# Fused adapter MLP, residual and gated FFN: the last down weight block, the first down parts and the first loads take other places

## The reference

```python
# x [8, 128, 512]; one of 16 adapters of rank 16 for each batch, SCALE = 0.5
gate = x @ W_gate.T + SCALE * (x @ A_gate[i].T) @ B_gate[i].T      # 1376 wide
up   = x @ W_up.T   + SCALE * (x @ A_up[i].T)   @ B_up[i].T
act  = silu(gate) * up
y    = act @ W_down.T + SCALE * (act @ A_down[i].T) @ B_down[i].T  # 512 wide
nx   = y * rsqrt(mean(y * y) + 1e-5) * ln_w
out  = x + (silu(nx @ gate_w.T) * (nx @ up_w.T)) @ down_w.T        # 1792 wide
```

## Time and profile before

| | us |
|---|---|
| median of 3 runs | 421.85 (421.34 to 421.91) |
| the profiled execution | 418.57 |
| its span in the trace | 416.8 |
| TensorE busy | 407.8 (98%) |
| VectorE busy | 320.4 (77%) |
| ScalarE busy | 234.4 (56%) |
| GpSimd busy | 12.4 (3%) |

### The profile page before, as it was taken

The page is one execution under the profiler, slowest core; times in us unless marked ns, Lnnn a source line. Parts: engine busy times, 40 slices in busy tenths (PEclk is TensorE's granted clock), DMA queues, the critical chain, the costliest instruction groups (busy, mean ns, idle before and its releaser), DMA issues.

```text
span 416.8 us, 5390 instructions
## 1 busy us (share of the span) xinstructions
PE 407.8 (98%) x1826; PEld 336.3 (81%) x1826; DVE 320.4 (77%) x493; ACT 234.4 (56%) x369; POOL 12.4 (3%) x16
## 2 busy tenths in 40 slices
PE   7999999999999999999999999999999999899996
PEld 5888888888887888888878888888888888688885
DVE  3899877777784748553889988788787868899993
ACT  4597666565654348641755464555655382574740
POOL 9000000000000200000000000000000000000000
PEclk9999999999999999999999999999999999999999
DMA  7630134311110340210010223131331125105112
GB/s 256 197 103 0 59 109 115 118 50 50 52 50 28 98 130 2 59 43 0 4 48 3 79 71 101 52 101 50 103 92 59 52 89 199 42 0 190 50 50 102
DMA packets 13965, 31.87 MB, mean 76 GB/s; under 512 B 2290, under 2 KB 4722, under 8 KB 13938
## 3 DMA queue, kind: packets, MB, share of 16 engines
q1 hardware_dynamic: 13426, 30.88, 23.0%
q10 hardware_dynamic: 512, 0.66, 0.6%
HBM read 29.43 MB, written 2.10 MB: 76 GB/s over the span
## 4 chain that ended last, share of the span: by engine, by line
PE 89%; DVE 3%; DMA 2%; issue 2%; ACT 2%; ACTq 0%; DVEq 0%
PE bank L1270 42%; PE bank L1446 14%; PE bank L1581 13%; PE bank L1374 10%; PE bank L1459 2%; PE bank L1404 2%; PE bank L1280 2%; ACT stack L378 2%; DMA xsum_c<-wsh_in 1%; PE bank L1411 1%; DVE xs L788 1%; DMA wdr<-vs_in 1%; DVE act L831 1%; PE bank L1466 0%; DVE wdr L903 0%
## 5 line engine op out<-in xcount | busy, mean ns | idle before, releaser
L1270 PE MATMUL bank<-xs,ws 128*128 128x512 f32 x840 | 194.8, 390 | 0.3
L1270 PEld LDWEIGHTS bank<-xs,ws 128*128 128x128 f32 x840 | 156.4, 188 | 33.2 <-DVE act L831 1.5
L1446 PE MATMUL bank<-xs,wdc 128*128 128x512 f32 x264 | 63.0, 390 | 0.5 <-DVE xs L788 0.5
L1446 PEld LDWEIGHTS bank<-xs,wdc 128*128 128x128 f32 x264 | 49.2, 188 | 10.9 <-issue 0.9
L378 ACT ACTIVATE xs<-act 128x512 fp32r<-128x512 f32 x71 | 42.9, 623 | 19.0 <-DVE act L938 7.6
L788 DVE TENSOR_TENSOR xs<-act,xs 128x512 fp32r<-128x512 f32 x71 | 47.8, 686 | 6.4 <-ACT xs L378 5.8
L1374 PE MATMUL bank<-xs,ws 128*128 128x512 f32 x192 | 44.8, 390 | 0.0
L788 DVE TENSOR_TENSOR ws<-wraw,ws 128x256 fp32r<-128x256 f32 (+1 forms) x49 | 32.9, 682 | 14.2 <-ACT ws L378 14.1
L1374 PEld LDWEIGHTS bank<-xs,ws 128*128 128x128 f32 x192 | 35.7, 188 | 7.2
L1581 PE MATMUL bank<-xs,vs 128*128 128x512 f32 x168 | 38.5, 390 | 1.5 <-DVE xs L788 1.5
L378 ACT ACTIVATE bank<-bank 128x512 f32<-128x512 f32 x22 | 12.7, 580 | 45.7 <-PE bank L1270 45.7
(11 more groups left out here) (113 smaller groups left out, 398.2 us busy)
## 6 DMA issues: line engine op xcount, KB each, us to landing
wraw<-wgu_in SPq DMA_DIRECT2D x24, 512.0 KB, 3.3
wdr<-vs_in SPq DMA_DIRECT2D x7, 512.0 KB, 3.5
wdr<-wd_in SPq DMA_DIRECT2D x11, 256.0 KB, 2.6
wraw<-vj_in SPq DMA_DIRECT2D x3, 896.0 KB, 4.5
xa<-xT_in SPq DMA_DIRECT2D x3, 512.0 KB, 7.1
bgu_raw<-bgu_in SPq DMA_DIRECT2D x32, 32.0 KB, 1.9
xres<-xT_in SPq DMA_DIRECT2D x4, 256.0 KB, 3.8
act<-xT_in SPq DMA_DIRECT2D x4, 256.0 KB, 6.0
```

What stands on the lines that cost most here:

```text
L1270: ins = mm(z[:, :], ws[:, j % 2, w, s, k * P:(k + 1) * P], xs[:, c, r, k, :], start=(start and k == 0 and s == 0 and r == 0), stop=(k == 1 ...
L1446: ins = mm(z[:, :], wd[:, s, h * P:(h + 1) * P], x[r], start=(start and s == 0 and r == 0), stop=False, skip_group_check=True)
```

## The change

Four places are edited.

- WARM goes from 10 to 8.
- Loads: the first channel tile of the first token half goes as one transfer of 128 partitions at the head of SP's queue, not as two halves on SP's and ScalarE's queues; idx goes out after the four tiles of xa0; ScalarE issues the transfer of the remaining short weights behind its first activation, which brings the table load with it.
- In group(j), the split of the first conditioning down weight part and operand stands ahead of c11; this matters only in the last conditioning group, j = 7.
- FFN down: hi_v(6) on ScalarE, and sums_v(6) and lo_v(6) on VectorE, stand behind item 13, the last of product 1, and not between items 8 and 10.

```diff
-WARM = 10
+WARM = 8
...
-            sp.dma_start(xa0[0:64, 0, :], xT_in[0, 0:64, 0, :]).then_inc(s_x0_ld[0], 16)
-            sp.dma_start(idx[:, :], idx_in[:, :]).then_inc(s_idx, 16)
+            sp.dma_start(xa0[:, 0, :], xT_in[0, :, 0, :]).then_inc(s_x0_ld[0], 16)
             sp.dma_start(xa0[:, 1, :], xT_in[0, :, 1, :]).then_inc(s_x0_ld[1], 16)
             sp.dma_start(xa0[:, 2:4, :], xT_in[0, :, 2:4, :]).then_inc(s_x0_ld[2], 16)
+            sp.dma_start(idx[:, :], idx_in[:, :]).then_inc(s_idx, 16)
...
             nc.scalar.dma_start(wsh_raw[:, 0], wsh_in[:, 0]).then_inc(s_wsh_ld[0], 16)
-            nc.scalar.dma_start(xa0[64:P, 0, :], xT_in[0, 64:P, 0, :]).then_inc(s_x0_ld[0], 16)
-            nc.scalar.dma_start(wsh_raw[:, 1:KT], wsh_in[:, 1:KT]).then_inc(s_wsh_ld[1], 16)
             a.wait_ge(s_warm, 2)
             silu(stat[:, 1:2], stat[:, 0:1]).then_inc(s_table, 1)
+            nc.scalar.dma_start(wsh_raw[:, 1:KT], wsh_in[:, 1:KT]).then_inc(s_wsh_ld[1], 16)
...
                 if i == 3:
                     hi_v(KF - 2)
-                elif i == KF + 2:
-                    hi_v(KF - 1)
...
                 hi_down(i)
+                if i == 2 * KF - 1:
+                    hi_v(KF - 1)
...
-                if j % 2 == 1:
-                    c11(j)
                 if j == S1 - 1:
                     lo_wd(0)
                     lo_ac(0)
+                if j % 2 == 1:
+                    c11(j)
...
-                elif i == KF + 1:
+                elif i == 2 * KF - 1:
                     sums_v(KF - 1)
-                elif i == KF + 3:
                     lo_v(KF - 1)
```

More of the change, by code:

```diff
@@ L623, in _ @@
             nc.scalar.dma_start(wsh_raw[:, 0], wsh_in[:, 0]).then_inc(s_wsh_ld[0], 16)
-            nc.scalar.dma_start(xa0[64:P, 0, :], xT_in[0, 64:P, 0, :]).then_inc(s_x0_ld[0], 16)
-            nc.scalar.dma_start(wsh_raw[:, 1:KT], wsh_in[:, 1:KT]).then_inc(s_wsh_ld[1], 16)
             a.wait_ge(s_warm, 2)
             silu(stat[:, 1:2], stat[:, 0:1]).then_inc(s_table, 1)
+            nc.scalar.dma_start(wsh_raw[:, 1:KT], wsh_in[:, 1:KT]).then_inc(s_wsh_ld[1], 16)
             for k in range(KT):
                 if k < 3:
-                    a.wait_ge(s_x0_ld[k], 32 if k == 0 else 16)
+                    a.wait_ge(s_x0_ld[k], 16)
                 copy(xs[:, (X11, X21)[k // 2], 0, k % 2, :], xa0[:, k, :]).then_inc(s_xhi[0], 1)
```

## The result

| | before | after |
|---|---|---|
| median of 9 runs, us | 421.34 (419.4 to 423.4) | 418.38 (418.09 to 419.31) |
| ratio of the times, 95% interval | | 0.9936 (0.9916 to 0.9957) |
| profiled execution, us | 418.57 | 419.01 |
| its span, us | 416.8 | 417.2 |

By the ratio the changed kernel is 0.64% faster, 2.7 us. Ratios and intervals leave out the few slow executions, over 1.5% longer than the fastest of their kernel; medians are of all executions, so that a quotient of medians can differ from the ratio beside it.

What follows compares the result with a forecast made beforehand. TensorE, busy 407.8 of 416.8 us, was taken as the bound, so only 9.0 us of idleness could be won. Terms -1.53 - 0.47 + 1.2 = -0.8 us took the median from 421.85 to 421.05, range 419.2 to 422.5.

Steps and rivals of the forecast that it cites:

- The last down weight block: FFN down: moving block 6 behind the fourteenth operand removes TensorE's wait at item 9, with no new wait; -1.53 us.
- The first down parts: Last conditioning group: lo parts split in VectorE's idle time before the gate product, removing TensorE's wait at L1446; -0.47 us.
- The start: Late indices delay SP's gathers by 1.8 us, so L1411 starts at 20.1 instead of 18.89; +1.2 us, bounds -0.59 and +2.65.
- The index wait: Start: indices queued behind all four tiles land at 7.25 us, so SP's gathers start 1.8 us later.
- Off the path, 0: Start: eight warm-up matmuls end at about 4.75 us, before the first operand's earlier arrival at 5.86, so dropping two costs nothing.
- the short projection ends 0 to 1.2 us sooner: Start: the remaining short weights land up to 1.2 us sooner, or unchanged, so the projection ends that much before 18.89.
- the clock as a rival at 0.09: TensorE's idle gap before L1411 drops the clock to 1.2 GHz, losing 1.8 us: +1.0, 422.85 us; chance 0.09.
- the short warm-up as one of two in 0.05: Start: eight warm-ups fail to raise the clock, first products lose up to 1.8 us; chance 0.05 shared with block 6.
- The sum and the median: Whole kernel: the terms sum to -0.8 us, taking the profiled execution from 418.57 to 417.8 and the median to 421.05.
- and I apply the difference there: The median 421.85 lies 3.3 us above the profiled execution, so the -0.8 us is applied to the median: 421.05.
- Indices not late: Rival: the queue serves the index transfer early, the start gives up to -0.59, sum -2.6, 419.3 us; chance 0.2.
- the rival for the other side: The slower-side clock rival: clock falls in the gap before L1411, +1.0, 422.85 us; chance 0.09.

Runs made afterwards that it cites:

- the run with the index second: Changed kernel with the index transfer back in second place of SP's queue: 418.73 us, ratio 0.9934 to the kernel before.
- the three sets: Follow-up runs in sets of four, each set on its own chip beside the unchanged kernel before, which took 420.63, 420.18 and 421.95 us.
- the second measurement: The changed kernel once more, no edit, against the kernel before: 419.39 us beside 420.63, ratio 0.9964.

## Why the prediction was wrong, step by step

**The last down weight block, -1.53 us.** The mechanism was right in each step: splits to 13 first, item 9 without a wait, block 6 with 2.2 us of cover, no later wait. The size was off: -1.84. **The first down parts, -0.47**: right, but -0.73. Both for the same reason. I took the idle time in the timeline's brackets. A bracket counts from the end of a matmul, but where TensorE runs through, matmuls overlap: one of L1446 lasts 0.39 us and the next starts 0.23 us after it. A wait loses these 0.16 us of overlap too, and the first matmul behind it lasts 0.47 us (L1446) or 0.50 (L1581). In the chain the twelve of L1446 behind the wait take 2.96 us before and 2.72 after, and 240 behind the wait at 358.43 take 54.72 us, where at the 0.2267 us of the changed kernel they would take 54.4. So each removed wait gave 0.25 to 0.3 us on top, 2.57 in place of 2.00. That is the trace of one execution; by the times the two edits give 3.5 us.

**The start, +1.2 us.** The index wait came as worked out: 2.2 us on SP, the first gather at 8.04 (8.2 in the text), the gathers' parts at 19.46 (19.96). But it did not set the start of L1409. Two steps that I had put aside did. "Off the path, 0" for the warm-up and "the short projection ends 0 to 1.2 us sooner" both fail: it ended 3.0 us later in the first pair of traces, 2.0 in the mean of the traces. The first weights landed at 5.1 and not at 2.8, although their own issue had not moved; their cast then met the memset; and the clock was at 1.2 GHz for the first eight to thirteen matmuls. I had the clock as a rival at 0.09, at the wrong gap (before L1411, not before the first product), and the short warm-up as one of two in 0.05; that one named the right matmuls, but with the new loads ten warm-up matmuls did not help either. Nowhere in the text is the cast. So +1.2 came out near the +1.9 to 2.0 of the times and traces by luck: the late index behind it cost nothing in the changed kernel, as the run with the index second shows (0.9934 against 0.9936 and 0.9964).

**The sum and the median.** This is the step that missed the range. Against a clean execution of before the sum was not bad: 418.57 was to become 417.8, and by the traces it is -2.57 + 2.0 = -0.6 us against the -0.8 that I added up, since by luck the errors of the start and of the stages nearly cancel. I wrote that the median is 3.3 us above the profiled execution "and I apply the difference there", as if these 3.3 us were an offset that both kernels have. They are not. In part they were the chance of three runs: 421.85 became 421.34 with nine, and 420.18 to 421.95 in the three sets. For the rest, about half of the executions of before lose 2 us or more at a lower mean clock, and the runs show that this loss goes with the two waits that the stage edits remove: with the old start 60 of 117 executions have the low clock with the waits and 1 of 13 without, and the spread falls from 3.7 us and more to 2.5 and less. The times of the same edits, 3.5 us in two sets against 2.57 in the traces, fit, though their intervals would not show it alone. The term that I put at nothing is what the removed waits are worth in the executions that are not clean, by this estimate about 1 us of the mean (half of them, 2 us each). With it, -3.5 + 1.9 = -1.6 us is the -1.5 of the second measurement; the first, -2.7, lies 1.2 us lower, and the intervals of the two overlap.

**The rivals.** "Indices not late" gave 419.3 and was nearest to the result, for a wrong reason: the indices were late. The clock fell, at another gap than the rival for the other side had it, and the kernel was faster all the same.

**Open**: where in the long executions of before the clock falls. The only trace that shows it fall with the old loads is of the kernel with 8 warm-up matmuls, and there it falls in the start; the pattern of the times points at the later stages. Also why the first short weights land 2.3 us later when SP's first transfer carries 256 KB and not 128.

## What to carry to other kernels

Before a difference is applied to a median, look at whether the profiled execution is a typical one: compare its time and its mean clock with the runs, and if the runs fall in groups, ask which group each edit touches. Here the group that mattered was touched by the edits far from the start: a wait of TensorE cost its own length in the clean execution and more in the others. Before a transfer or a warm-up is called off the path, look at what else runs beside the instruction that uses it, on other engines too: the cast took 2.74 us here where it takes 0.26 alone. And price a removed wait by the chain from product to product, not by the idle bracket.

## What the runs showed of the hardware

- A VectorE cast of 128x192 took 0.26 us alone (two traces) and 2.36 to 2.77 us in the six traces where it met GpSimd's memset of 32x3072, ending each time 0.11 to 0.12 us behind the memset. Subtractions of two inputs of 128x512 beside GpSimd's memsets kept the 0.68 to 0.69 us that they take elsewhere.
- 96 KB issued on ScalarE's queue at 0.83 us had landed by 2.8 to 3.4 in the six traces with the old loads (128 KB at the head of SP's queue) and by 5.1 to 5.5 in the eight with the new ones (256 KB there). The two orders differ in more than this size, so the cause is not shown.
- In the run with the new loads alone the clock was granted in full 2.65 us after the last warm-up matmul, and fell 1.2 us after the first product's start, with matmuls running. With the stage edits alone it stayed full through 2.61 us of idleness after the six first matmuls. In the changed kernel's first trace the granted clock reads 1.00 from 8 to 12 us, while its matmuls last 0.63 us as at the low clock: their length is the safer witness.
- A matmul of 128x512 lasted 0.39 us in steady flow while the next started 0.2267 us after it; the first behind a wait of 0.47 us lasted 0.47, behind one of 1.53 us 0.50.
